# Layer 0 context attention: TensorE's program written out instead of looped, and value products for four head pairs at a time

## What is computed

```python
q = split_heads(x @ Wq) * 64 ** -0.5          # 16 heads
k, v = split(context @ Wkv)                   # then the null key and value in front
attn = softmax(q @ k.T)
out = (attn @ v).reshape(b, -1, 1024) @ Wout
out = (out - mean) * rsqrt(var + 1e-6) * ln_scale + ln_bias
x = x + out
```

## Time and profile before

| | |
|---|---|
| median of three runs | 4516.92 us (4514.62 to 4517.19) |
| the profiled execution's own time | 4519.83 us |
| its span in the trace | 4518.0 us |
| mean granted PE clock, share of full speed | 0.917 |
| PE busy, share of the span | 84% |
| DVE busy | 63% |
| ACT busy | 44% |
| DMA queue 1 (data), share of 16 engines | 27.3% |

### The profile page before, as it was taken

One profiled execution on the slowest core, in us unless ns is written; L12 is line 12 of the kernel. 1 busy time (PEld: TensorE's weight loads), 2 busy tenths in 40 slices (PEclk: granted clock), 3 DMA queues, 4 the chain that ended last, 5 costly groups with the idle time before them and its releaser, 6 DMA issues. The chain is left out here.

```text
span 4518.0 us, 116638 instructions
## 1 busy us (share of the span) xinstructions
PE 3780.1 (84%) x46470; PEld 2881.3 (64%) x46470; DVE 2838.7 (63%) x5431; ACT 1998.1 (44%) x4327; POOL 818.4 (18%) x797
## 2 busy tenths in 40 slices
PE   5999999999999873279998679889997777879776
PEld 4888888888888642257666356656664345656454
DVE  2766666666666587442223776567776956878683
ACT  2332333233223364533333333478887745654323
POOL 0000000000000041200000036555553012200160
PEclk7999999999999986689999889989998989989878
DMA  4655555555555145310000023222220000000000
GB/s 127 133 120 119 120 119 120 120 120 120 119 119 123 39 125 183 123 70 1 0 0 21 5 101 145 79 71 67 72 71 27 0 6 3 0 13 1 9 3 24
DMA packets 307757, 320.58 MB, mean 71 GB/s; under 512 B 43440, under 2 KB 295249, under 8 KB 299873
## 3 DMA queue, kind: packets, MB, share of 16 engines
q1 hardware_dynamic: 307296, 313.84, 27.3%
HBM read 286.44 MB, written 27.05 MB: 69 GB/s over the span
## 5 line engine op out<-in xcount | busy, mean ns | idle before, releaser
L3891 PE MATMUL c_psA<-c_kc,c_qt 128*128 128x257 f32 x2048 | 497.6, 398 | 78.0 <-issue 77.4
L3912 PEld LDWEIGHTS c_psB<-c_pt,c_vc 32*128 32x128 f32 x16384 | 471.8, 188 | 44.5 <-issue 44.5
L3912 PE MATMUL c_psB<-c_pt,c_vc 32*128 32x128 f32 x16384 | 496.2, 274 | 1.9 <-DVE c_vo L4091 1.9
L3891 PEld LDWEIGHTS c_psA<-c_kc,c_qt 128*128 128x128 f32 x2048 | 399.9, 201 | 139.5 <-issue 81.3
L4015 ACT ACTIVATE c_sc<-c_psA,c_mx 128x257 f32<-128x257 f32 x512 | 215.4, 473 | 534.4 <-DVE c_mx L4102 534.4
L637 PEld LDWEIGHTS f_psY<-f_w_down,f_hT 128*128 128x128 f32 x2560 | 302.7, 192 | 64.7 <-issue 48.4
L680 ACT ACTIVATE f_hT<-f_psH,f_b_up 128x512 f32<-128x512 f32 x320 | 214.3, 688 | 281.1 <-PE f_psH L627 276.5
L4098 DVE TENSOR_REDUCE c_nm<-c_psA 128x2 f32<-128x514 f32 x256 | 176.7, 690 | 255.8 <-PE c_psA L3891 255.8
L627 PE MATMUL f_psH<-f_xs,f_w_up 128*128 128x512 f32 x640 | 303.6, 610 | 17.3 <-ACT f_hT L680 17.3
L637 PE MATMUL f_psY<-f_w_down,f_hT 128*128 128x128 f32 x2560 | 306.9, 276 | 10.1 <-ACT f_hT L680 5.7
L2320 POOL TENSOR_TENSOR x_sc<-x_sc,x_rec 128x1156 f32<-128x1156 f32 x128 | 270.7, 2115 | 208.0 <-DVE x_rec L2586 208.0
(11 more groups left out here) (823 smaller groups left out, 7695.4 us busy)
## 6 DMA issues: line engine op xcount, KB each, us to landing
c_vc<-in_ctx SPq DMA_DIRECT2D x512, 256.0 KB
c_kc<-in_ctxT SPq DMA_DIRECT2D x128, 257.0 KB
g_wide<-g_w_dram SPq DMA_DIRECT2D x32, 1024.0 KB, 8.3
x_kc<-in_ctxT SPq DMA_DIRECT2D x32, 512.0 KB
x_vc<-in_ctx SPq DMA_DIRECT2D x64, 256.0 KB
l_k_dram<-l_dist SPq DMA_DIRECT2D x32, 256.0 KB, 4.3
l_q_dram<-l_turn SPq DMA_DIRECT2D x8, 1024.0 KB, 9.7
y_pt<-l_q_dram SPq DMA_DIRECT2D x8, 1024.0 KB, 5.9
```

The lines of the kernel that those rows point to most:

```text
L3891: mm = pe.matmul(psA[:, r, 0:KEYS], qt[:, b // BT, half * BT + b % BT, r * G:(r + 1) * G].rearrange("p h i -> p (h i)"), kc[:, b // 2 % 2, ...
L3912: mm = pe.matmul(psB[:, e, half * P:(half + 1) * P], vc[e * S:(e + 1) * S, b % 4, t, half * P:(half + 1) * P], pt[e * S:(e + 1) * S, :, t] ...
```

## The change

It has two parts. PE's loop over chunks 1 to 14 becomes a Python loop, so that PE's whole stage is one straight program; the loops of DVE, ACT, SP and POOL stay. And `head_values` now takes four head pairs (32 matmuls of the trace) at the odd batches of a chunk and nothing at the even ones, where it took two pairs (16) at each. DVE's copy to `c_vo` goes with it: 128x512 at odd batches in place of 128x256 at each. The counts that wait for these copies (`values_read`, in `context` and `output`) are halved, and `output` now waits itself for DVE's copy of the context product (`ot_ready["dve"]`), a wait that stood ahead of the values at the same batch.

```diff
--- before.py
+++ after.py
@@ -3751,6 +3751,12 @@
 
             return FILLS if last and b >= BT else i * NB + b + FIRST
 
+        def values_before(m, b, first):
+
+            if first and b < BT + 2:
+                return None
+            return 2 * (m - 1) + (b % BT) // 2
+
         with nc.Block() as block:
             @block.sync
             def _(sp):
@@ -3916,17 +3922,17 @@
 
                 def head_values(bank, s, j):
 
-                    for a in range(2):
+                    for a in range(4):
                         for half in range(2):
                             for e in range(2):
-                                h = (2 * j + a) * 2 + e
+                                h = (4 * j + a) * 2 + e
                                 mm = pe.matmul(bank[e * DV:(e + 1) * DV, a * P:(a + 1) * P], wv[:, half, h],
                                                ot[:, s, half * G + h // G, h % G].rearrange("p b i -> p (b i)"),
                                                start=(half == 0), stop=(half == 1))
                     mm.then_inc(values_in, 1)
 
                 def output(m, s):
-                    pe.wait_ge(values_read, (m + 1) * 4)
+                    pe.wait_ge(values_read, (m + 1) * 2)
                     pe.wait_ge(lz_ready, m + 1)
                     pe.wait_ge(wn_loaded[s], (m - s) * 32 + 64)
                     pe.nop(nofuse=True)
@@ -3943,7 +3949,7 @@
                         if not (first and b == 0):
                             c = (b - 1) % NB
                             context(n - 1, c, i * 2 + (b - 1) // 4 + 1,
-                                    n - 4 if not (first and b <= 4) else None,
+                                    values_before(m, b, first),
                                     min(n + 2, FILLS - FIRST + 1) if last else n + 2,
                                     m - 1 if b % BT == 1 and not first else None, first and b == 1)
                         if not (last and s == 1):
@@ -3953,12 +3959,13 @@
                             fill(psA, b % BT)
                         if not (first and b == 0):
                             pe.wait_ge(ot_ready["act"], n)
-                        if not (first and s == 0):
-                            if b % BT == 0:
+                        if b % 2 and not (first and s == 0):
+                            if b % BT == 1:
                                 pe.wait_ge(ot_ready["dve"], n)
                             pe.nop(nofuse=True)
-                            head_values(psB[:, 1], 1 - s, b % BT)
+                            head_values(psB[:, 1], 1 - s, b % BT // 2)
                         if b % BT == 0 and not first:
+                            pe.wait_ge(ot_ready["dve"], n)
                             output(m - 2, s)
                         if not (last and (s == 1 or b == BT - 1)):
                             to = (b + 1) % BT
@@ -3989,15 +3996,15 @@
                 pe.wait_ge(fixed, 9 * 16)
                 pe.wait_ge(values_loaded, 48)
                 chunk(0, True, False)
-                with pe.Fori(1, NI - 1) as i:
+                for i in range(1, NI - 1):
                     chunk(i, False, False)
                 chunk(NI - 1, False, True)
-                context(B - 1, NB - 1, NG, B - BT, FILLS - FIRST + 1, None)
+                context(B - 1, NB - 1, NG, 2 * (NG - 1), FILLS - FIRST + 1, None)
                 pe.wait_ge(exp_done, B * EX)
                 for e in ("act", "dve"):
                     pe.wait_ge(ot_ready[e], B)
                 output(NG - 2, 0)
-                for j in range(4):
+                for j in range(2):
                     head_values(psA[:, j], 1, j)
                 pe.wait_ge(out_read, NG - 1)
                 output(NG - 1, 1)
@@ -4088,7 +4095,7 @@
                     v.wait_ge(values_in, f + 1)
                     if j == 0 and not opening:
                         v.wait_ge(out_done, m)
-                    v.tensor_copy(vo[:, 2 * j:2 * j + 2].rearrange("p a t -> p (a t)"), bank[:, 0:2 * P])\
+                    v.tensor_copy(vo[:, 4 * j:4 * j + 4].rearrange("p a t -> p (a t)"), bank)\
                         .then_inc(values_read, 1)
 
                 def maxima(i, b):
@@ -4141,8 +4148,8 @@
                         if not (last and s == 1):
                             take_queries(psA, n + FIRST, 1 - s, b % BT)
                         scale_and_turn(n, b, first)
-                        if not (first and s == 0):
-                            take_values(psB[:, 1], n - BT, m - 1, b % BT, first)
+                        if b % 2 and not (first and s == 0):
+                            take_values(psB[:, 1], 2 * (m - 1) + b % BT // 2, m - 1, b % BT // 2, first)
                         if b % BT == 2 and not first:
                             count_out(m - 2)
 
@@ -4158,8 +4165,8 @@
                 chunk(NI - 1, False, True)
                 take_contexts(B - 1, NB - 1)
                 turn_tail(NG - 1, 1)
-                for j in range(4):
-                    take_values(psA[:, j], B - BT + j, NG - 1, j)
+                for j in range(2):
+                    take_values(psA[:, j], 2 * (NG - 1) + j, NG - 1, j)
                 count_out(NG - 2)
                 count_out(NG - 1)
 
```

## The result

The changed kernel takes 4437.86 us (median of four runs; 4426.51 to 4441.23) against 4515.79 of the kernel before, also in four runs: a ratio of 0.982, with a 95% interval of 0.981 to 0.984, or 78 us less. The forecast was 4440. The profiled execution took 4436.19 us, with a span of 4434.4, against 4519.83 and 4518.0.

What follows compares the result with a forecast made beforehand. PE was taken to set the pace, idle at 13 loop branches. From the profiled 4519.83 us, -81.4 (branches), +4 (values) and +0.6 (stage end) gave 4443.0, so 4440 us was forecast, range 4427 to 4466.

Steps and rivals of the forecast that it cites:

- the 81.4 us: PE's 13 loop boundaries: writing the loop out saves 53.5 us idle plus 27.9 us of slow matmuls.
- The values: Value products moved to odd batches: +0.12 us per group of four batches, +4 us over thirty groups.
- -1.02, +1.74 and -0.60: Per group: batch 0 without values, two odd batches with 16 more matmuls each, batch 2 without values but waiting.
- Who is queued behind: Other engines' copies, transposes, loads and waits behind the moved values: all fit, with 1.3 us slack for DVE's transpose.
- the first rival: Chunk ends: DVE's or ACT's branch comes to light, 26 us, giving 4466 us; chance 8%.
- The end of the stage: Last context product and last output: each waits 0.3 us longer for wider copies, +0.6 us.
- The sum: Profiled execution: 4519.83 - 81.4 + 4 + 0.6 = 4443.0 us, so a forecast of 4440 us.
- Small waits: Rival at batch 2 of each group: the waits let the clock fall, 64 us, giving 4504 us; chance 3%.
- The gap was the branch's: Chunk ends: the idle time belongs to the branch; the rival denied it, giving 4521 us, no change; chance 3%.
- Straight code: Rival in PE's written-out program: late instruction fetches stall it, one per group giving 4629 us; chance 2%.
- The idle time ahead of the context products: Rival in PE's loop: this idle time goes with the register instructions, 37.6 us, giving 4402 us; chance 2%.

Runs made afterwards that it cites:

- the straight program alone: Kernel before with only PE's loop over chunks 1 to 14 written out, values left at every batch: 4438.0 us, ratio 0.982.
- six for six: Changed kernel with chunks 1 to 14 as a PE loop of seven rounds, two chunks each, six branches back: 4488.4 us, ratio 0.994.
- branches that jump nowhere: Changed kernel with each of chunks 1 to 14 in a PE loop that runs once: 4439.2 us, ratio 0.982.
- a body that PE holds: Kernel before with 3 of 8 key tiles in the context product, about 1670 matmuls and loads per loop body: 4294 us, part of the result left out.
- the kernel that stood still without a branch: Changed kernel with PE waiting at each chunk start for DVE's values copy, which DVE repeats three times more: 4529.4 us, ratio 1.0018.
- the values alone: Changed kernel with PE's loop put back, so only the values move to odd batches: 4545.7 us, ratio 1.007.
- the later load: Kernel before with SP's context load of each chunk's last batch issued some 5 us later: 4502.8 us, ratio 0.996.

## Why the prediction was right

**The bound and the 81.4 us.** The step "it removes 13 taken branches, and so the 81.4 us, if the gap belongs to the branch" held to 1.4 us: the straight program alone has a range of 1179.7 us, where 1259.7 less 81.4 is 1178.3. The condition in it was argued from chunk 0 and 15 and is now shown: gaps go by taken branch (six for six), disappear with branches that jump nowhere, disappear with a body that PE holds, and are covered by the branch instructions' own 3.6 to 5.7 us. Both halves of the price are shown too, the idle time by the fetch and the slow matmuls by the kernel that stood still without a branch.

**The values.** -1.02, +1.74 and -0.60 per group gave +0.12; the rows give 42.22 - 42.08 = +0.14. The wait at the third batch and its 0.20 us are there. This held only because the loop went at the same time: inside the loop the same wait is 0.46 us. I had priced it from chunk 0, which is straight code, so the price was right for the forecast and would have been wrong for the values alone: 18.6 us in the trace, and 27 between the medians, against my 3.

**Who is queued behind.** DVE's transpose ends 1.3 us ahead of the context product at a batch without values, as worked out: no wait of PE for `c_pt`, `c_sc` or `c_mx` stands in the waits of the changed kernel. The other engines' branches did not come to light, so the first rival is refuted; DVE's, in the changed kernel, take at most 76 ns each:

```profile
L4163 DVEq COMPARE_BRANCH  x14: 50/56/76, 256.6 to 1354.5; - x14
```

**The end of the stage.** "+0.6" is the mis-sized term. From the scores of batch 120 to the last output the stage takes 93.8 us in place of 97.1: -3.3. The copies are longer as forecast, about 0.3 us each time, but the last context product ran at the full clock (2.8 us), and the batches of the last chunk took 1.0 us less. The forecast put the clock at this place at nothing. It is in part luck that it came out as a gain: the same product behind the old wait took 6.64, 5.48 and 3.85 us in three kernels.

**The sum.** 4443.0 us were forecast for the profiled execution, 4436.2 came. The end of the stage explains 4 us of that, chunk 0 another 1.5, and 2.7 are the first scores beginning at 93.9 us in place of 96.5. Against them stand 0.7 us in the loop's range and 1.1 in the stages behind. Chunk 0 and the start are not the change's: in a second trace of the changed kernel chunk 0 takes 80.6 us in place of 78.6, with its first scores at 6.50 us in place of 5.56, and in all traces here, looped and straight, the stage's first scores begin either at 93.4 to 94.0 or at 96.5 to 97.4 us. That the median fell within 2 us of the forecast of 4440 is in part luck: medians of the kernel before lay between 4515 and 4523 on the chips of the experiments.

**The rivals.** Small waits did not let the clock fall: 28 of 0.20 us in the range, and the clock at 1.00. The gap was the branch's, by the experiments above. Straight code did not stall once in 1182 us, with the DMA engines at 0.59; it needs 166 / 14 = 11.9 packets per chunk, where the forecast had read about 14 from a loop that fetched some of them twice. The idle time ahead of the context products did not go.

## What to carry to other kernels

Before unrolling or rolling a loop on TensorE, count the instructions of its body. Here a body of about 1770 was as good as free to loop, and bodies of about 2280 and more paid for each branch back with 2.5 to 6 us of idle time, and then mostly again with matmuls at a lower clock; straight code paid nothing. Where between the two sizes the border lies no run here shows. Look for that price in the trace as idle time with no releaser that recurs once per round, and include the slow matmuls behind it, a third of the whole here. And price a second edit in the program in which it will stand: moving the value products was nearly free in the straight program and cost 0.7% in the loop (0.4% by the trace), where a wait and the gaps at the branches grew with it.

## What the runs showed that I had not expected

A wait of PE for the copy of the fill costs 0.46 to 0.48 us in the looped parts of programs and 0.20 in straight ones, with the same matmuls around it and register instructions between them only in the loops. A gap of some 2.5 to 3.5 us does not always lower the clock: behind the 13 gaps of 2.5 to 3.7 us with the later load it held three times (3.71 us for the scores) and fell ten times, and so it did again with the values moved as well. The length of the idle time alone doesn't decide: the three that held took 2.50, 2.54 and 3.03 us, and behind another of 2.50 it fell. What does decide stays open, at the last context product too, which ran 6.64, 5.48 and 3.85 us behind the same wait of 1.95 us.
